# Two-layer graph attention kernel: row statistics moved between engines, and the bias row fed to the matmul as bf16 parts

## The chip, the cores and the metric

The kernel runs on one core of one Trainium2 chip. The metric is the device time of one execution in microseconds, the median of several runs. A core has five engines that work side by side, each through its own list of instructions in order: TensorE (PE in the profile, with its weight loads as PEld), VectorE (DVE), ScalarE (ACT), GpSimd (POOL) and SyncE (SP), which issues DMAs. Engines wait for one another through semaphores.

## The reference

`x` is 2048 x 256, `adj` is a 2048 x 2048 matrix of zeros and ones, sparse except for its first rows. Both layers have 8 heads of 32 columns.

```python
def _layernorm(x, axis=-1, eps=1e-05):
    m = jnp.mean(x, axis=axis, keepdims=True)
    v = jnp.var(x, axis=axis, keepdims=True)
    return (x - m) / jnp.sqrt(v + eps)
...
# layer 0
scores = jnp.einsum('hnd,hmd->hnm', q, k)
scores = jnp.where(adj > 0, scores, NEG_FILL)
attn = jax.nn.softmax(scores, axis=-1)
out = jnp.einsum('hnm,hmd->hnd', attn, vv)
...
# layer 1
h = (x @ W_w.T + W_b).reshape(Bn, H, D)
e = jax.nn.leaky_relu(s_src[:, None, :] + s_dst[None, :, :], negative_slope=0.2)
e = jnp.where(adj[:, :, None] == 0, jnp.float32(-1000000000.0), e)
attn = jax.nn.softmax(e, axis=1)
h_prime = jnp.einsum('ijh,jhd->ihd', attn, h).reshape(Bn, H * D)
return jax.nn.elu(h_prime)
...
x = _layernorm(x + _L0_gnn_ref(x, L0_gnn_x2, L0_gnn_v, adj), axis=-1)
x = _layernorm(x + _L1_gnn_ref(x, adj, L1_gnn_W_w, L1_gnn_W_b, L1_gnn_a), axis=-1)
```

What the change touches is the statistics of the two LayerNorms and the bias `W_b` in the projection `h`.

## The kernel before

The kernel never builds the dense attention. It turns `adj` into lists of edges, gathers for each edge the row of its neighbour, and adds the weighted rows up with matmuls against 0/1 selection matrices. The 2048 rows are 16 tiles of 128, taken in 7 groups; `k` from 0 to 15 is a tile's place in that order. A tile's edges are cut into chunks of 128 edges, 78 chunks in all. VectorE extracts the lists (`MAX8` on L1381, and the lines around it), GpSimd issues one indirect DMA per chunk (L965) into a ring of buffers of 24 slots in layer 0 and 44 in layer 1, VectorE scores and weighs the gathered rows (L1510, L1514, L1566), and TensorE sums them into a tile's rows (L1313). Layer 1 gathers from a table in memory that layer 0 writes. So its first gather waits for the last tile of layer 0 to be stored, while the lists are used again.

What a tile of layer 0 does when its sums are there (`tile_stages`, L314): VectorE divides by the softmax denominators (L1350, L1352), adds `x` (L1573), takes mean and variance with two statistics instructions (L1342, L1344) and adds eps to the variance (L1577). GpSimd raises that to the power -0.5 and forms the shift -mean * rstd (L983, L985). ScalarE writes the normed rows (L1134). TensorE turns them (L1319), ScalarE copies them out (L1141), and TensorE projects them: two instructions for the bias row times a row of ones (L1326), then four for the two halves of the weights (L1328); one source line of fp32 matmul shows as two instructions. ScalarE evacuates (L1148), SyncE stores to the table (L907), GpSimd adds to a column sum and splits the source scores in three bf16 parts (L1025 to L1039).

A tile of layer 1: divide, ELU on ScalarE (L1152, L1155), VectorE finishes the ELU (L1587), adds `x` (L1589) and takes the two statistics instructions; for every pair of tiles ScalarE makes a first guess of rstd (L1162, L1164), VectorE refines it in four small instructions (L1597 to L1603), ScalarE emits the two tiles (L1170).

The order of the work on each engine is fixed when the program is built. `all_stages` (L202) names some 1160 stages, each with an engine, a time in us, a rank and the stages it follows; `Order.flat` (L162) plays this list through once, always taking the startable stage of lowest rank, and every engine's program is written in the order that comes out. A changed time in a `put` can move any stage behind it, on all engines.

At the start SyncE loads the weights in 22 DMAs after the first four tiles of `adj` (L888 to L897), the bias row as one of them (L893); TensorE multiplies them (`sum_w`, L1229, L1231) when all have landed, and ScalarE copies the result (L1118, L1119), among it the last columns of `b_row`. The tile `e_w_sb` that held the weights is not used after that.

Of the kernel before, what the change touches and what calls it, by code (L numbers as in the profile page):

```python
# [14 lines left out]
P = 128  # L15
H = 8
# [185 lines left out]
def all_stages(plan):  # L202
# [111 lines left out]
    def tile_stages(layer, k, rank):  # L314
        end = last_sums(layer, k)
        if layer == 0:
            put("DVE", 2.1, rank - 0.2, ("norm", k), end, ("x", plan.group_of_k(k)), ("normed", k - 4) if k >= 4 else None)
            put("POOL", 1.1, rank - 0.3, ("shift", k), ("norm", k))
# [3 lines left out]
            put("PE", 2.0, rank - 0.2, ("project", k), ("copy_norm", k), ("evac", k - 1) if k else ("copy_mean", 0))  # L322
# [3 lines left out]
        else:  # L326
            put("DVE", 0.7, rank - 0.2, ("norm_a", k), end, ("emit", k - 4) if k >= 4 else ("normed", NK - 4 + k))
            put("ACT", 0.9, rank - 0.3, ("elu", k), ("norm_a", k), ("norm_b", k - 2) if k >= 2 else None)
            put("DVE", 1.6, rank - 0.2, ("norm_b", k), ("elu", k))
            if k % 2:  # L330
                put("ACT", 0.5, rank - 0.3, ("guess", k // 2), ("norm_b", k))
                put("DVE", 0.8, rank - 0.3, ("refine", k // 2), ("guess", k // 2))
# [347 lines left out]
def edge_pass(nc, x, adj, kv, w_nat, wT, w_b, a, out, table, needed, out_stored):  # L680
# [15 lines left out]
    with ExitStack() as ctx:  # L696
        def sb(name, shape, dt=F32):
            return ctx.enter_context(nc.sbuf_tensor(name, shape, dt))
# [24 lines left out]
        w_sb = sb("e_w_sb", [P, 2, C])  # L723
        w_ext = sb("e_w_ext", [P, 2, CX])
        b_row = sb("e_b_row", [1, CX])
# [69 lines left out]
        stats = sb("e_stats", [P, 6])  # L795
        mv = sb("e_mv", [P, 4, 2])
# [72 lines left out]
        def _(sp):  # L869
# [23 lines left out]
            sp.dma_start(b_row[:, 0:CV].rearrange("p (h e) -> p h e", e=D1)[:, :, 0:D], w_b.rearrange("(a h d) -> a h d", a=1, d=D)).then_inc(s("w_loaded"), 16)  # L893
# [22 lines left out]
        def _(pool):  # L916
# [35 lines left out]
            for stage in stages:  # L952
# [25 lines left out]
                elif stage[0] == "shift":  # L978
# [3 lines left out]
                    at_least(pool, "normed", k - 3)  # L982
                    own.did(nc.gpsimd.tensor_tensor(rstd[:, one], var_eps[:, one], minus_half[:], ALU.pow))  # L983
                    own.wait()
                    nc.gpsimd.tensor_scalar(shift[:, one], mv[:, k % 4, 0:1], rstd[:, one], -1.0, ALU.mult, ALU.mult).then_inc(s("shift_ready"), 1)  # L985
# [58 lines left out]
        def _(act):  # L1044
# [3 lines left out]
            for stage in stages:  # L1048
# [66 lines left out]
                elif stage[0] == "copy_w":  # L1115
# [3 lines left out]
                    nc.scalar.copy(b_row[:, CV:CX], pj[0:1, 4 * H:6 * H]).then_inc(s("w_ready"), 1)  # L1119
# [4 lines left out]
                elif stage[0] == "exp":  # L1124
# [5 lines left out]
                    nc.scalar.activation(weight_t[0:CH, :], shifted[0:CH, :], ACT.Exp, scale=SCALE if layer == 0 else 1.0).then_inc(s("exp_ready"), 1)  # L1130
                elif stage[0] == "normed":
# [25 lines left out]
                elif stage[0] == "guess":  # L1157
# [3 lines left out]
                    act.wait_ge(s("var_ready"), NT + 2 * j + 2)  # L1161
                    own.did(nc.scalar.activation(log_var[:, two], mv[:, two, 1], ACT.Ln, bias=eps[:]))  # L1162
# [11 lines left out]
        def _(pe):  # L1174
            for stage in stages:
# [48 lines left out]
                elif stage[0] == "sum_w":  # L1224
                    pe.wait_ge(s("const_ready"), N_CONST)
                    pe.wait_ge(s("w_loaded"), 16 * (6 + 2 * H))
# [3 lines left out]
                    for o in range(2):  # L1230
                        last = nc.tensor.matmul(pj[0:1, 4 * H:6 * H], b_col[:, o:o + 1], a_diag[:, o, :], start=(o == 0), stop=(o == 1))  # L1231
# [89 lines left out]
                elif stage[0] == "project":  # L1321
# [4 lines left out]
                    nc.tensor.matmul(pj[:, 0:CX], ones[0:1, :], b_row[:], start=True, stop=False)  # L1326
# [10 lines left out]
        def _(dve):  # L1337
# [3 lines left out]
            def moments(k):  # L1341
                st.did(v.bn_stats(stats[:], y[:, k % 4, :]))  # L1342
                st.wait()
                return v.bn_aggr(mv[:, k % 4, :], stats[:])  # L1344
# [10 lines left out]
            for stage in stages:  # L1355
# [212 lines left out]
                elif stage[0] == "norm":  # L1568
# [81 lines left out]
```

## Time and profile before

| | |
|---|---|
| median of 3 runs | 498.96 us (497.28 to 499.59) |
| the profiled execution's own time | 500.55 us |
| its span, first to last instruction | 498.9 us |
| granted TensorE clock, mean | 0.714 of full |
| PE busy | 277.4 us, 56% |
| DVE busy | 314.6 us, 63% |
| ACT busy | 157.2 us, 32% |
| POOL busy | 239.6 us, 48% |
| PEld busy | 193.7 us, 39% |

The share of busy time is a mean over stages that differ: list extraction and layer 0 share the first 300 us, and the gathers and sums of layer 1 fill the rest. A granted clock of 1.0 is 2.4 GHz and of 0.5 is 1.2 GHz; means between the two are mixtures. Idle time in a view names what ended it; "remote" is a release for which the profile has no instruction on this core.

### The profile page before, as it was taken

How to read it: one execution, taken by the hardware profiler on the slowest of the kernel's cores; microseconds unless marked ns; L12 is line 12 of the kernel's file. 1: busy time of each engine (PE TensorE's matmuls, PEld its weight loads, DVE VectorE, ACT ScalarE, POOL GpSimd, SP SyncE). 2: the span in 40 equal slices, each digit the busy share in tenths (PEclk: the TensorE clock that was granted, in tenths of full speed). 3: DMA queues.
4: the chain of work that ended last, by engine and by line, in shares of the span. 5: the costliest groups of instructions: out<-in, count | busy, mean ns of one | idle time of the engine just before them, and what ended most of it. 6: DMA issues, size and time to landing. Idle time of an engine off the chain costs nothing.

```text
span 498.9 us, 5673 instructions
## 1 busy us (share of the span) xinstructions
PE 277.4 (56%) x1506; PEld 193.7 (39%) x1506; DVE 314.6 (63%) x870; ACT 157.2 (32%) x352; POOL 239.6 (48%) x383
## 2 busy tenths in 40 slices
PE   0338676447755865886898875230004535595680
PEld 0226443335433543654556543120003423373450
DVE  3997988999978996996836620300014345677773
ACT  6433745325343334233221222000010022535322
POOL 7453746572478574478461335777742726000000
PEclk9859785969566995797755975575555957676796
DMA  8886567275277233154022002444431424101001
GB/s 308 266 266 233 213 206 262 57 284 169 97 198 228 109 88 107 43 135 125 1 68 84 12 24 67 112 112 112 112 78 28 113 60 109 45 1 43 21 1 47
DMA packets 24484, 57.94 MB, mean 116 GB/s; under 512 B 6560, under 2 KB 14880, under 8 KB 22400
## 3 DMA queue, kind: packets, MB, share of 16 engines
q0 software_dynamic: 10032, 31.77, 22.9%
q1 hardware_dynamic: 14416, 25.76, 14.9%
q8 instruction: 13, 0.21, 0.2%
q14 instruction: 23, 0.19, 0.1%
HBM read 53.19 MB, written 4.33 MB: 115 GB/s over the span
## 4 chain that ended last, share of the span: by engine, by line
PE 20%; another core or an unknown queue 16%; DVE 12%; issue 7%; POOL 3%; ACT 3%; DVEq 0%; ACTq 0%; POOLq 0%
PE e_po L1313 10%; PE e_pj L1328 2%; DVE e_weighted L1566 2%; PE e_pj L1326 1%; PE e_po L1297 1%; ACT e_sel_edges L1109 1%; DVE e_stats L1342 1%; PE e_pt L1222 1%; PE e_pq L1257 1%; POOL e_ring L965 1%; DVE e_y L1352 1%; DVE e_y L1589 1%; DVE e_y L1587 1%; POOL e_rstd L983 1%
## 5 line engine op out<-in xcount | busy, mean ns | idle before, releaser
L1313 PE MATMUL e_po<-e_weighted,e_sel_edges 128*128 128x264 f32 x312 | 100.9, 483 | 17.1 <-DVE e_weighted L1566 13.7
L965 POOL DMA_INDIRECT e_ring<-table,e_col_i x78 | 74.0, 948 | 45.2 <-DVE e_weighted L1566 22.3
L965 POOL DMA_INDIRECT e_ring<-in_kv,e_col_i x78 | 77.9, 998 | 34.6 <-issue 20.6
L1313 PEld LDWEIGHTS e_po<-e_weighted,e_sel_edges 128*128 128x128 f32 x312 | 73.2, 243 | 38.9 <-DVE e_weighted L1566 19.3
L1109 ACT COPY e_sel_edges<-e_pt 128x512 f32<-128x512 f32 (+3 forms) x45 | 23.6, 524 | 98.2 <-remote 53.3
L1222 PE MATMUL e_pt<-e_identb,e_sel_rows 128*128 128x128 bf16 x156 | 21.4, 273 | 44.9 <-ACT e_sel_edges L1109 31.1
L1566 DVE TENSOR_TENSOR e_weighted<-e_ring,e_pc 128x528 f32<-128x528 f32 (+1 forms) x55 | 35.6, 684 | 14.6 <-PE e_po L1313 9.5
L1257 PE MATMUL e_pq<-e_parts,e_sel_rows 128*128 128x256 bf16 x234 | 43.7, 351 | 1.0 <-DVE e_prod L1510 1.0
L1297 PE MATMUL e_po<-e_mean_row,e_diagonal 128*128 128x264 f32 x64 | 24.4, 474 | 35.3 <-issue 21.4
L1381 DVE MAX8 e_raw<-e_vals 128x8 bf16<-128x256 bf16 (+1 forms) x88 | 41.5, 513 | 1.0
L1222 PEld LDWEIGHTS e_pt<-e_identb,e_sel_rows 128*128 128x128 bf16 x156 | 14.1, 120 | 54.3 <-issue 52.5
L1053 ACT ACTIVATE e_vals<-e_adj 128x2048 bf16<-128x2048 int32 x16 | 30.6, 1911 | 14.5 <-DVE e_raw L1381 7.2
L1510 DVE TENSOR_TENSOR e_prod<-e_pq,e_ring 128x512 f32<-128x512 f32 (+1 forms) x40 | 25.6, 672 | 14.5 <-PE e_pq L1257 9.0
L1257 PEld LDWEIGHTS e_pq<-e_parts,e_sel_rows 128*128 128x128 bf16 x234 | 28.0, 124 | 10.2 <-DVE e_prod L1510 1.1
L1350 DVE RECIPROCAL e_rden<-e_po 128x8 f32<-128x8 f32 x32 | 6.5, 204 | 40.2 <-remote 32.6
L1297 PEld LDWEIGHTS e_po<-e_mean_row,e_diagonal 128*128 128x128 f32 x64 | 12.3, 222 | 39.6 <-issue 37.9
L1514 DVE TENSOR_REDUCE e_score<-e_prod 128x16 f32<-128x512 f32 (+1 forms) x40 | 24.9, 663 | 0.1
L1366 DVE TENSOR_TENSOR e_vals<-e_vals,e_code 128x2048 bf16<-128x2048 bf16 x16 | 19.5, 1219 | 8.1 <-ACT e_vals L1053 8.0
L983 POOL TENSOR_TENSOR e_rstd<-e_var_eps,e_minus_half 128x1 f32<-128x1 f32 x16 | 9.9, 618 | 30.4 <-DVE e_var_eps L1577 28.0
L1566 DVE TENSOR_TENSOR e_weighted<-e_ring,e_pl 128x528 f32<-128x528 f32 (+1 forms) x25 | 16.5, 688 | 9.6 <-PE e_po L1313 5.8
L1076 ACT ACTIVATE e_diagonal<-e_ident,e_filled 128x128 f32<-128x128 f32 x32 | 12.4, 395 | 19.2 <-issue 8.8
L1134 ACT ACTIVATE e_xres<-e_y,e_shift,e_rstd 128x256 f32<-128x256 f32 x16 | 9.6, 598 | 24.4 <-POOL e_shift L985 24.4
(184 smaller groups left out, 534.0 us busy)
## 6 DMA issues: line engine op xcount, KB each, us to landing
e_adj<-in_adj SPq DMA_DIRECT2D x16, 1024.0 KB
table<-e_hx SPq DMA_DIRECT2D x16, 136.0 KB
e_ring<-in_kv SPq DMA_DIRECT2D x1, 2112.0 KB, 13.1
out<-e_prod SPq DMA_DIRECT2D x16, 128.0 KB, 1.7
e_ring<-in_kv,e_col_i POOLq DMA_INDIRECT x78
e_ring<-table,e_col_i POOLq DMA_INDIRECT x78
e_xres<-in_x SPq DMA_DIRECT2D x2, 512.0 KB
e_xres<-in_x SPq DMA_DIRECT2D x3, 256.0 KB, 12.0
```

The costliest lines, as they stand in the source:

```text
L965: nc.gpsimd.indirect_dma_start(out=rings[layer][:, q % RING[layer], :], out_offset=None, in_=kv if layer == 0 else table, in_offset=bass.I ...
L1053: nc.scalar.activation(vals[:, k % 2, :], adj_tile[:, k % 2, :], ACT.Sign, accum_out=signs[:, k:k + 1]).then_inc(s("sgn_ready"), 1)
L1109: nc.scalar.copy(sel_edges[:, n % TURNED:n % TURNED + m, :].rearrange("p c r -> p (c r)"), pt[:, 0:m * P]).then_inc(s("turns_copied"), 1)
L1222: last = nc.tensor.matmul(pt[:, j * P:(j + 1) * P], sel(q + j), identb[:], start=True, stop=True)
L1257: last = nc.tensor.matmul(pq[b % 2][:, j * C:(j + 1) * C], sel(q0 + c0 + j), parts[:, g % 2, at, part, :], start=(part == 0), stop=(part = ...
L1297: nc.tensor.matmul(po[n % 2][:, 0:CV], diagonal[:, n % 2, :], mean_row[:], start=True, stop=False).then_inc(s("sums_begun"), 1)
L1313: nc.tensor.matmul(po[n % 2][:, 0:CV], sel_edges[:, (layer * plan.n_chunks + q) % TURNED, :], weighted[:, b % 3, j * CV:(j + 1) * CV], sta ...
L1366: st.did(v.tensor_tensor(tile_vals, tile_vals, code[:].bitcast(BF16), ALU.mult))
L1381: last = v.max(raw[:, i * TOP:(i + 1) * TOP], segs[:, i])
L1510: v.tensor_tensor(prod[:, i % 2, 0:m * C].rearrange("p (c k) -> p c k", c=m), pq[b % 2][:, 0:m * C].rearrange("p (c k) -> p c k", c=m), ri ...
L1514: ins = v.tensor_reduce(score[:, n % 2, c0:c0 + m, :].rearrange("p c h -> p (c h)"), by_head(prod[:, i % 2, 0:m * C]), AX_X, ALU.add)
L1566: v.tensor_tensor(weighted[:, b % 3, 0:m * CV].rearrange("p (c h d) -> p c h d", c=m, d=D1), rings[layer][:, at:at + m, lo:lo + CV].rearra ...
```

## The change

Layer norm. VectorE's add of `x` becomes a `scalar_tensor_tensor` that also gives the row sum (`accum_out`), and its two statistics instructions and the eps addition are gone. ScalarE gets a new stage per tile (`spread_of` in layer 0, `spread_of_b` in layer 1): it scales the sum to -mean, and squares `y - mean` with an accumulated row sum. The squared rows themselves go to a buffer that is free then. GpSimd's `shift` has one more small instruction in layer 0 (eps and the division by 256), before the power. `refine` on VectorE keeps four instructions.

Bias. The bias row is loaded on three partitions instead of one (three DMAs for one), `sum_w` makes its last columns on three partitions, and a new GpSimd stage `split_b` replaces the three copies by three bf16 parts whose sum is the fp32 row. The buffers for it lie in `e_w_sb`. In `project`, one bf16 matmul with a contraction over three partitions stands for the fp32 one with a contraction over one.

Planned times of the stages that changed are edited with it.

```diff
     def tile_stages(layer, k, rank):
         end = last_sums(layer, k)
         if layer == 0:
-            put("DVE", 2.1, rank - 0.2, ("norm", k), end, ("x", plan.group_of_k(k)), ("normed", k - 4) if k >= 4 else None)
-            put("POOL", 1.1, rank - 0.3, ("shift", k), ("norm", k))
+            put("DVE", 1.35, rank - 0.2, ("norm", k), end, ("x", plan.group_of_k(k)), ("normed", k - 4) if k >= 4 else None)
+            put("ACT", 1.0, rank - 0.3, ("spread_of", k), ("norm", k), ("project", k - 2) if k >= 2 else None)
+            put("POOL", 1.4, rank - 0.3, ("shift", k), ("spread_of", k))
...
-            put("PE", 2.0, rank - 0.2, ("project", k), ("copy_norm", k), ("evac", k - 1) if k else ("copy_mean", 0))
+            put("PE", 1.6, rank - 0.2, ("project", k), ("copy_norm", k), ("evac", k - 1) if k else ("copy_mean", 0))
...
-            put("DVE", 1.6, rank - 0.2, ("norm_b", k), ("elu", k))
+            put("DVE", 1.05, rank - 0.2, ("norm_b", k), ("elu", k))
+            put("ACT", 1.0, rank - 0.3, ("spread_of_b", k), ("norm_b", k))
             if k % 2:
-                put("ACT", 0.5, rank - 0.3, ("guess", k // 2), ("norm_b", k))
+                put("ACT", 0.5, rank - 0.3, ("guess", k // 2), ("spread_of_b", k))
...
     put("ACT", 0.7, 0.0, ("copy_w",), ("sum_w",))
+    put("POOL", 1.7, 0.0, ("split_b",), ("copy_w",))
...
-            sp.dma_start(b_row[:, 0:CV].rearrange("p (h e) -> p h e", e=D1)[:, :, 0:D], w_b.rearrange("(a h d) -> a h d", a=1, d=D)).then_inc(s("w_loaded"), 16)
+            for p in range(3):
+                sp.dma_start(b_row[p:p + 1, 0:CV].rearrange("p (h e) -> p h e", e=D1)[:, :, 0:D], w_b.rearrange("(a h d) -> a h d", a=1, d=D)).then_inc(s("w_loaded"), 16)
...
                     pool.wait_ge(s("var_ready"), k + 1)
                     at_least(pool, "normed", k - 3)
+                    own.did(nc.gpsimd.tensor_scalar(var_eps[:, one], squares[:, one], 1.0 / C, EPS, ALU.mult, ALU.add))
+                    own.wait()
                     own.did(nc.gpsimd.tensor_tensor(rstd[:, one], var_eps[:, one], minus_half[:], ALU.pow))
                     own.wait()
-                    nc.gpsimd.tensor_scalar(shift[:, one], mv[:, k % 4, 0:1], rstd[:, one], -1.0, ALU.mult, ALU.mult).then_inc(s("shift_ready"), 1)
+                    nc.gpsimd.tensor_tensor(shift[:, one], neg_mean[:, one], rstd[:, one], ALU.mult).then_inc(s("shift_ready"), 1)
+                elif stage[0] == "split_b":
+                    pool.wait_ge(s("w_ready"), 3)
+                    own.did(nc.gpsimd.tensor_scalar(less[:, 0:1], part_no[0:3, :], 0.5, -1.0, ALU.is_gt, ALU.mult))
+                    own.did(nc.gpsimd.tensor_scalar(less[:, 1:2], part_no[0:3, :], 1.5, -1.0, ALU.is_gt, ALU.mult))
+                    own.did(nc.gpsimd.memset(onesb, 1.0))
+                    for j in range(2):
+                        own.did(nc.gpsimd.tensor_copy(b_parts, b_row[:]))
+                        own.wait()
+                        own.did(nc.gpsimd.tensor_scalar(b_less, b_parts, less[:, j:j + 1], None, ALU.mult))
+                        own.wait()
+                        own.did(nc.gpsimd.tensor_tensor(b_row[:], b_row[:], b_less, ALU.add))
+                        own.wait()
+                    nc.gpsimd.tensor_copy(b_parts, b_row[:]).then_inc(s("bias_split"), 1)
...
+                elif stage[0] == "spread_of":
+                    k = stage[1]
+                    one = slice(k % 4, k % 4 + 1)
+                    act.wait_ge(s("z_ready"), k + 1)
+                    at_least(act, "h_summed", k - 1)
+                    if k == 1:
+                        act.wait_ge(s("rank_ready"), 1)
+                    own.did(nc.scalar.activation(neg_mean[:, one], total[:, one], ACT.Copy, scale=-1.0 / C))
+                    own.wait()
+                    nc.scalar.activation(xts[k % 2][:], y[:, k % 4, :], ACT.Square, bias=neg_mean[:, one], accum_out=squares[:, one]).then_inc(s("var_ready"), 1)
+                    act.wait_ge(s("var_ready"), k + 1)
+                elif stage[0] == "spread_of_b":
+                    k = stage[1]
+                    one = slice(k % 4, k % 4 + 1)
+                    act.wait_ge(s("z_ready"), NT + k + 1)
+                    own.did(nc.scalar.activation(neg_mean[:, one], total[:, one], ACT.Copy, scale=-1.0 / C))
+                    own.wait()
+                    nc.scalar.activation(elu[:, k % 2, :], y[:, k % 4, :], ACT.Square, bias=neg_mean[:, one], accum_out=squares[:, one]).then_inc(s("var_ready"), 1)
+                    act.wait_ge(s("var_ready"), NT + k + 1)
...
-                    nc.tensor.matmul(pj[:, 0:CX], ones[0:1, :], b_row[:], start=True, stop=False)
+                    if k == 0:
+                        pe.wait_ge(s("bias_split"), 1)
+                    nc.tensor.matmul(pj[:, 0:CX], onesb, b_parts, start=True, stop=False)
...
-            def moments(k):
-                st.did(v.bn_stats(stats[:], y[:, k % 4, :]))
-                st.wait()
-                return v.bn_aggr(mv[:, k % 4, :], stats[:])
+            def with_x(k):
+                return v.scalar_tensor_tensor(out=y[:, k % 4, :], in0=y[:, k % 4, :], scalar=1.0, in1=xres[:, k, :],
+                                              op0=ALU.mult, op1=ALU.add, accum_out=total[:, k % 4:k % 4 + 1])
...
-                    st.did(v.tensor_tensor(y[:, k % 4, :], y[:, k % 4, :], xres[:, k, :], ALU.add))
-                    st.wait()
-                    st.did(moments(k))
-                    st.wait()
-                    v.tensor_scalar(var_eps[:, k % 4:k % 4 + 1], mv[:, k % 4, 1:2], EPS, None, ALU.add).then_inc(s("var_ready"), 1)
+                    with_x(k).then_inc(s("z_ready"), 1)
...
-                    st.did(v.tensor_tensor(y[:, k % 4, :], y[:, k % 4, :], xres[:, k, :], ALU.add))
-                    st.wait()
-                    moments(k).then_inc(s("var_ready"), 1)
-                    dve.wait_ge(s("var_ready"), NT + k + 1)
+                    with_x(k).then_inc(s("z_ready"), 1)
```

## Rows read from the trace of the kernel before

**Rows 1.** The page's chain of work that ended last, shares by line

```profile
PE e_po L1313 10%; PE e_pj L1328 2%; DVE e_weighted L1566 2%; PE e_pj L1326 1%; PE e_po L1297 1%; ACT e_sel_edges L1109 1%; DVE e_stats L1342 1%; PE e_pt L1222 1%; PE e_pq L1257 1%; POOL e_ring L965 1%; DVE e_y L1352 1%; DVE e_y L1589 1%; DVE e_y L1587 1%; POOL e_rstd L983 1%
```

**Rows 2.** Stretches: length, busy us (instructions) by engine, then clock, DMA share, GB/s

```profile
50.00:200.00 150.00, 92.49 (x620) 63.87 (x617) 131.16 (x348) 66.14 (x139) 89.00 (x118) 0.75 0.52 168
...
250.00:275.00 25.00, 21.90 (x109) 14.44 (x109) 11.89 (x23) 5.15 (x12) 9.41 (x18) 0.50 0.27 76
275.00:304.00 29.00, 22.88 (x117) 14.66 (x117) 11.83 (x34) 8.55 (x21) 9.52 (x28) 0.79 0.06 20
304.00:422.00 118.00, 37.55 (x148) 27.09 (x146) 29.06 (x71) 12.16 (x31) 73.61 (x78) 0.60 0.36 93
422.00:499.00 77.00, 43.09 (x158) 30.54 (x158) 51.19 (x149) 28.85 (x74) 0.35 (x1) 0.72 0.09 28
```

**Rows 3.** Timeline (start us, length us), layer 1: a late release and POOL's two ring waits

```profile
351.47 0.21 DVE L1350 RECIPROCAL e_rden<-e_po 128x8 f32<-128x8 f32 x1 [26.15 <-remote]
...
382.28 0.94 POOL L965 DMA_INDIRECT e_ring<-table,e_col_i  x1 [13.22 <-DVE e_weighted L1566]
...
410.16 0.94 POOL L965 DMA_INDIRECT e_ring<-table,e_col_i  x1 [8.19 <-DVE e_weighted L1566]
```

**Rows 4.** Timeline of VectorE: the add of x, and what starts when its norm ends

```profile
214.19 0.43 DVE L1573 TENSOR_TENSOR e_y<-e_y,e_xres 128x256 f32<-128x256 f32 x1
...
215.41 0.21 DVE L1350 RECIPROCAL e_rden<-e_po 128x8 f32<-128x8 f32 x1
...
222.48 0.42 DVE L1573 TENSOR_TENSOR e_y<-e_y,e_xres 128x256 f32<-128x256 f32 x1
...
487.32 0.42 DVE L1589 TENSOR_TENSOR e_y<-e_y,e_xres 128x256 f32<-128x256 f32 x1
...
488.46 0.43 DVE L1587 SCALAR_TENSOR_TENSOR e_y<-e_prod,e_y 128x256 f32<-128x256 f32 x1
```

**Rows 5.** Groups of instructions: busy us, mean ns of one, idle before and releaser

```profile
L1491 DVE SCALAR_TENSOR_TENSOR e_hit<-e_slot_e,e_rel 128x256 f32<-128x256 f32 x16 | 8.3, 517 | 1.5 <-ACT e_slot_e L1098 0.4
L1491 DVE DVE_READ_ACCUMULATOR e_hit<-e_slot_e,e_rel 128x1 f32 x16 | 1.3, 81 | 0.0
L1059 ACT ACTIVATE e_half<-e_signs 128x2 f32<-128x2 f32 (+2 forms) x7 | 1.4, 197 | 0.1
L1152 ACT ACTIVATE e_left<-e_y 128x256 f32<-128x256 f32 x16 | 6.6, 413 | 27.9 <-DVE e_y L1352 27.9
L1053 ACT ACTIVATION_READ_ACCUMULATOR e_vals<-e_adj 128x1 f32 x16 | 3.0, 188 | 0.0
L985 POOL TENSOR_SCALAR e_shift<-e_mv,e_rstd 128x1 f32<-128x1 f32 x16 | 5.4, 339 | 1.6
L1029 POOL TENSOR_TENSOR e_h_sum<-e_h_sum,e_hx 128x264 f32<-128x264 f32 x15 | 11.6, 773 | 0.0
```

**Rows 6.** Timeline of TensorE around the projection of one tile, clock 0.5

```profile
245.94 1.49 PE L1257 MATMUL e_pq<-e_parts,e_sel_rows 128*128 128x256 bf16 x6
247.36 1.30 PE L1326 MATMUL e_pj<-e_b_row,e_ones 1*128 1x280 f32 x2
248.58 2.24 PE L1328 MATMUL e_pj<-e_w_ext,e_xt 128*128 128x280 f32 x4
```

**Rows 7.** Pieces of the chain that ended last: start us, us, what

```profile
231.72 1.27 PE e_pj L1326 x2
...
283.81 0.70 PE e_pj L1326 x2
```

**Rows 8.** Timeline of the start: weight loads and who waits for them

```profile
17.96 2.98 SPq L893 DMA_DIRECT2D e_b_row<-in_w_b  x1
...
28.09 0.42 SPq L897 DMA_DIRECT2D e_a_diag<-in_a  x1
...
32.47 1.86 PE L1229 MATMUL e_pj<-e_a_diag,e_w_sb 128*128 128x16 f32 x8 [8.47 <-DMA e_a_diag<-in_a]
...
40.67 1.63 POOL L1001 TENSOR_SCALAR e_flags<-e_rel 128x128 bf16<-128x128 f32 x1 [7.05 <-DVE e_rel_end L1468]
```

More of the change, by code:

```diff
@@ L723, in edge_pass @@
         w_sb = sb("e_w_sb", [P, 2, C])
+        w_flat = w_sb[0:3].rearrange("p k c -> p (k c)")
+        b_less = w_flat[:, 0:CX]
+        b_parts = w_flat[:, CX:CX + CX // 2].bitcast(BF16)
+        onesb = w_flat[:, CX + CX // 2:CX + CX // 2 + P // 2].bitcast(BF16)
+        less = w_flat[:, 2 * C - 2:2 * C]
         w_ext = sb("e_w_ext", [P, 2, CX])
-        b_row = sb("e_b_row", [1, CX])
+        b_row = sb("e_b_row", [3, CX])
         b_col = sb("e_b_col", [P, 2])
@@ L794, in edge_pass @@
         xts = [sb("e_xt", [P, C]), count0]
-        stats = sb("e_stats", [P, 6])
-        mv = sb("e_mv", [P, 4, 2])
+        norms = sb("e_norms", [P, 3, 4])
+        total, neg_mean, squares = norms[:, 0, :], norms[:, 1, :], norms[:, 2, :]
         var_eps = sb("e_var_eps", [P, 4])
@@ L1118, in _ @@
                         nc.scalar.copy(w_ext[:, k, CV:CX], pj[:, k * 2 * H:(k + 1) * 2 * H]).then_inc(s("w_ready"), 1)
-                    nc.scalar.copy(b_row[:, CV:CX], pj[0:1, 4 * H:6 * H]).then_inc(s("w_ready"), 1)
+                    nc.scalar.copy(b_row[:, CV:CX], pj[0:3, 4 * H:6 * H]).then_inc(s("w_ready"), 1)
                 elif stage[0] == "copy_mean":
@@ L1160, in _ @@
                     act.wait_ge(s("const_ready"), N_CONST)
-                    act.wait_ge(s("var_ready"), NT + 2 * j + 2)
-                    own.did(nc.scalar.activation(log_var[:, two], mv[:, two, 1], ACT.Ln, bias=eps[:]))
+                    own.did(nc.scalar.activation(log_var[:, two], squares[:, two], ACT.Ln, bias=eps[:], scale=1.0 / C))
                     own.wait()
@@ L1225, in _ @@
                     pe.wait_ge(s("const_ready"), N_CONST)
-                    pe.wait_ge(s("w_loaded"), 16 * (6 + 2 * H))
+                    pe.wait_ge(s("w_loaded"), 16 * (8 + 2 * H))
                     for k in range(2):
@@ L1230, in _ @@
                     for o in range(2):
-                        last = nc.tensor.matmul(pj[0:1, 4 * H:6 * H], b_col[:, o:o + 1], a_diag[:, o, :], start=(o == 0), stop=(o == 1))
+                        last = nc.tensor.matmul(pj[0:3, 4 * H:6 * H], b_col[:, o:o + 1].to_broadcast([P, 3]), a_diag[:, o, :], start=(o == 0), stop=(o == 1))
                     last.then_inc(s("w_summed"), 1)
@@ L1596, in _ @@
                     dve.wait_ge(s("guess_ready"), j + 1)
-                    st.did(v.scalar_tensor_tensor(out=guessed[:, two], in0=mv[:, two, 1], scalar=EPS, in1=guess[:, two], op0=ALU.add, op1=ALU.mult))
+                    st.did(v.scalar_tensor_tensor(out=guessed[:, two], in0=squares[:, two], scalar=C * EPS, in1=guess[:, two], op0=ALU.add, op1=ALU.mult))
                     st.wait()
-                    st.did(v.scalar_tensor_tensor(out=guessed[:, two], in0=guessed[:, two], scalar=-0.5, in1=guess[:, two], op0=ALU.mult, op1=ALU.mult))
+                    st.did(v.scalar_tensor_tensor(out=guessed[:, two], in0=guessed[:, two], scalar=-0.5 / C, in1=guess[:, two], op0=ALU.mult, op1=ALU.mult))
                     st.wait()
@@ L1602, in _ @@
                     st.wait()
-                    v.scalar_tensor_tensor(out=shift[:, two], in0=mv[:, two, 0], scalar=-1.0, in1=rstd[:, two], op0=ALU.mult, op1=ALU.mult).then_inc(s("refined"), 1)
+                    v.tensor_tensor(shift[:, two], neg_mean[:, two], rstd[:, two], ALU.mult).then_inc(s("refined"), 1)
                     dve.wait_ge(s("refined"), j + 1)
```

## The prediction, made blind

> **What bounds the kernel now.** I read the page first: VectorE is busiest, and no engine is near its span. The chain of waits shows no single owner either; its largest line is the layer's sums on TensorE, L1313, with 10%, and the lines of this change (L1326, L1342, L983) have about 1% each [rows 1]. So I went by stretches. From 50 to 200 us VectorE is busy 131.16 of 150 us (87%) with the edge lists: it paces. From 250 to 304 it is TensorE, 21.90 of 25 us and then 22.88 of 29; the granted clock is 0.50 in the first part (1.2 GHz) and 0.79 in the second. From 304 to 422 GpSimd issues the 78 gathers of layer 1, 73.61 of 118 us, and the rest of that stretch is waiting. The tail, 422 to 499, is a mixture led by VectorE, 51.19 of 77 us (66%), with TensorE at 43.09 [rows 2]. In the gather stretch GpSimd stands twice for a free ring slot, 13.22 and 8.19 us, because VectorE's weighing is late; ahead of that VectorE stood 26.15 us for a release that the profile names remote [rows 3]. I can't explain that wait from the records, and it makes this stretch the least certain one.
>
> The profiled execution took 500.55 us: a span of 498.9 and 1.65 around it. The median of the runs is 498.96, 1.59 less. I sum against 500.55 and take 1.6 off at the end.
>
> **VectorE's part of the norm.** Before, layer 0 goes from the add's start at 214.19 to the next tile's reciprocal at 215.41: 1.22 us for the add, two statistics instructions and eps. Layer 1 takes 487.32 to 488.46, 1.14 us [rows 4]. After, one instruction stands there. The nearest is L1491, the same form and one accumulated output, 128x256 fp32: 0.517 with a read of 0.081 beside it, which I take together as 0.50 to 0.60; I use 0.50 [rows 5]. That saves 0.72 us per tile of layer 0 and 0.64 per tile of layer 1. Ten of the sixteen adds of layer 0 start by 222.48 [rows 4], where VectorE paces: 10 x 0.72 = 7.2, of which I count 70%, since VectorE was idle for 13% and some of the gain lands in such gaps: -5.0. Bounds: 0 and -7.2. In the tail VectorE's steps of layer 1 are on the chain: L1342 has 1% of it, about 5 us, which is some ten tiles at about the 0.43 of the add over the same 128x256 [rows 1, 4]. Eight tiles x 0.64 = -5.1, bounds 0 and -10.2 (all sixteen).
>
> **ScalarE's new step.** It waits for the add, scales the sum (0.197 by L1059), squares 128x256 (0.413 by L1152) and reads the accumulator (0.188 by L1053): 0.80, and 0.95 with the gaps. GpSimd has one more 128x1 instruction per tile of layer 0, 0.339 by L985 [rows 5]. One norm's latency in layer 0 so changes by +0.20 +0.41 +0.19 +0.34 -0.72 = +0.42, with a hand-over 0.5. The last six tiles of layer 0 lie where TensorE paces and their projection must end before layer 1 may gather. I let three of them show it and three show VectorE's gain: +1.5 -2.2 = -0.7. In layer 1 the first guess of rstd, one per pair of tiles, now waits for ScalarE's own two steps in place of VectorE's: 0.80 + hand-over against 0.64. I take 0.45 each for the last four pairs: +1.8. And 32 steps of 0.95 us (30.4 us) go in front of what ScalarE does for others: copies of turned edges, exponentials, evacuations. ScalarE is busy 66 of 150, 5 of 25, 29 of 77 us [rows 2], 20 to 44%. So a step meets other work of ScalarE about a third of the time, and I let a third of what it meets be on the path, as no engine owns more than that of the chain: 30.4/9 = +3.4. Bounds: 0, and +30.4 if every one is exposed. What waits behind the new step on ScalarE, while it waits for VectorE's add, are the list copies for VectorE and the selection matrices for TensorE; behind the guess, the emits alone.
>
> **Bias.** Around one projection at clock 0.5, six bf16 matmuls of 256 columns take 1.49 us, 0.25 each, and the two fp32 halves of the bias start 1.22 before the next, 247.36 to 248.58 [rows 6]. One bf16 matmul of 280 columns costs about 0.27: -0.95 per tile at this clock. On the chain there are six pairs of L1326 behind 230 us, five of 1.1 to 1.3 and one of 0.70, the first and that one shown in [rows 7]; at the higher clock I take -0.49. Sum 5 x 0.95 + 0.49 = -5.2, bounds 0 and -10 (six of them in full and the four before at 0.7).
>
> **Start.** Two more b_row DMAs stand on SyncE's list before the a_diag ones. The b_row row has 2.98 us, the a_diag row 0.42; TensorE waits 8.47 for the last a_diag, until 32.47 [rows 8]. I count the issue, 2 x 0.46 = +0.9; bounds 0 and 2 x 2.98 = +6.0. split_b is nine GpSimd instructions on three partitions; by the 128x264 row, 0.77 for a full-width one [rows 5], at most 4.3 us (three copies and two adds of 280 columns at 0.77, 3.9, and the rest small). It lies in GpSimd's wait of 7.05 us before 40.67 [rows 8]; if that cover is gone, up to +4.
>
> **Sum.** +0.9 -5.0 -0.7 -5.2 -5.1 +1.8 +3.4 = -9.9. 500.55 - 9.9 = 490.65, and 1.6 less is 489.1 us.
>
> **Rivals.**
> A, the other side: ScalarE becomes the pacer of each tile. Its program is in fixed order, and a step waiting for the add holds all behind it. At 0.95 a step, 20 of 32 exposed give +19.0 in place of +3.4, so the sum is -13.3 +19.0 = +5.7: 506.25 own, 504.7. The point from which it decides is 14 exposed steps (14 x 0.95 = 13.3). For it: every layer-0 step sits between list copies. Against: at most 44% busy.
> B, VectorE's savings are hidden: the lists in fact wait for DMA or ScalarE. Then start +0.9, bias -5.2 and +3.4 stay: -0.9, 498.1. Against: 87% busy [rows 2].
> C, the clock. 275 to 304 ran at 0.79, the 25 us before at 0.50 [rows 2]. With less work TensorE could stay at 0.50 there: 22.88 busy x (0.79/0.50 - 1) = 13.3 more, 80% of it on the path: +10.6, so 499.7. The Trainium skill, "TensorE: Matmul & The Clock Gate", section "Part 1: The HAM clock gate (the "warmup" mystery)", says that TensorE's clock is held down by default and raised by activity, by which less bias work would be a loss and not a gain. By this rule the time is that of C. The trace does not bear it out plainly: the clock is 0.50 where TensorE is 88% busy, and 0.72 in the tail with 56% [rows 2].
> D, the remote release. The order changes, and the 26.15 us wait may fall elsewhere; half of GpSimd's 21.4 us of ring waits [rows 3] goes (-10.7, 478.4) or comes again (+10.7, 499.8).
> That the change does not do what it says is small: one instruction for four on VectorE is in the diff.
>
> **How the numbers follow.** Chances: forecast 0.48, A 0.17, B 0.14, C 0.07, D downwards 0.09, upwards 0.05. The likeliest's own range is 482 to 495 (the bounds of the list stage, tail and ScalarE terms taken by half). The range over all cases is 476 to 504: the lower end takes in D's gain, the upper nearly all of A. What a measurement can tell from no change is about 0.5%, 2.5 us: 496.5 to 501.5. Faster: the forecast's 0.48, D's 0.09 and 0.04 of B, 0.61. Same: 0.09 of B, 0.03 of C, 0.03 of D upwards, 0.03 of A, 0.18. Slower: the other 0.14 of A, 0.04 of C, 0.02 of D, 0.01 of B, 0.21.
>
> **What would show it.** VectorE's groups: L1342, L1344, L1577 gone, one accumulating group of 32 at about 0.5. VectorE busy down by some 20 us, ScalarE's up by 26. The first layer-1 gather, at 304 before, near 294. L1326 at one instruction a tile, near 0.27 at clock 0.50. GpSimd's wait before its 40.67 instruction shorter and not its start later. In the tail, idle time of ScalarE before the square, and the guess released by ScalarE. I am wrong if the gather starts no earlier than 301, if ScalarE's new group is the releaser of waits on TensorE or VectorE that sum to over 10 us, or if the clock in the TensorE stretch falls to 0.5 throughout.

## The result: 475.1 us where 489.1 was forecast

The changed kernel took 475.12 us, median of four runs (472.72 to 479.47), where the kernel before took 498.66; the ratio is 0.954, interval 0.9465 to 0.9614. The direction was right. The size was not: the forecast was a gain of 9.9 us and the gain was 23.5, and 475.1 lies just below the stated range of 476 to 504. Its profiled execution took 475.88 us, with a span of 472.7. Here and below, times are medians of all executions of a kernel, while a ratio is taken over the fast executions alone, so that a difference of medians and a ratio can stand up to some 2 us apart.

The page of the changed kernel, busy time by engine and the chain of waits by line:

```profile
PE 259.2 (55%) x1490; PEld 184.4 (39%) x1490; DVE 294.7 (62%) x822; ACT 180.9 (38%) x448; POOL 249.1 (53%) x409
...
PE e_po L1355 11%; POOL e_ring L974 4%; PE e_pj L1372 3%; DVE e_weighted L1609 3%; PE e_pq L1299 3%; DVE e_raw L1424 3%; PE e_pj L1281 2%; DMA e_adj<-in_adj 1%; DVE e_score L1557 1%; ACT e_sel_edges L1133 1%; SPq L900 1%; POOL e_h_sum L1053 1%; ACT e_vals L1077 1%; DVE e_prod L1553 1%
```

VectorE is busy 294.7 us, 19.9 less than before. ScalarE has 180.9, 23.7 more, and TensorE 259.2, 18.2 less. The page's list of the chain has no line of the statistics or the bias any more. The projection (L1372) is still in it.

Stretches of the changed kernel (length; busy us and instructions of PE, PEld, DVE, ACT, POOL; then clock, DMA share, GB/s):

```profile
50.00:200.00 150.00, 98.57 (x644) 69.44 (x643) 132.89 (x353) 72.83 (x163) 94.36 (x128) 0.74 0.53 171
...
250.00:275.00 25.00, 18.51 (x79) 12.95 (x78) 14.28 (x33) 7.33 (x22) 6.41 (x18) 0.80 0.15 43
```

The list stage is as dense on VectorE as it was (132.89 of 150 us, 89%), as a stage would be that VectorE paces and that is over sooner. The 25 us that ran at 0.50 before run at 0.80 [rows 2]; they hold other work now, since layer 0 ends 17 us earlier.

Timeline of the same kernel at the places of the steps: GpSimd's first gather of layer 1, the two ring waits and the last gather:

```profile
286.94 1.06 POOL L974 DMA_INDIRECT e_ring<-table,e_col_i  x1 [0.89 <-DMA table<-e_hx]
...
365.25 0.95 POOL L974 DMA_INDIRECT e_ring<-table,e_col_i  x1 [13.37 <-DVE e_weighted L1609]
...
392.07 0.95 POOL L974 DMA_INDIRECT e_ring<-table,e_col_i  x1 [6.91 <-DVE e_weighted L1609]
...
403.75 0.94 POOL L974 DMA_INDIRECT e_ring<-table,e_col_i  x1 [0.30 <-issue]
```

The same two ends of the gather stretch in the kernel before:

```profile
304.13 1.04 POOL L965 DMA_INDIRECT e_ring<-table,e_col_i  x1 [0.90 <-DMA table<-e_hx]
...
421.41 0.95 POOL L965 DMA_INDIRECT e_ring<-table,e_col_i  x1 [0.30 <-issue]
```

The end of that span was at 498.9. So layer 0 gave 17.2 us, the gather stretch 0.5 (117.3 against 116.8), and the tail, which is what lies behind the last gather, 8.5 (77.5 against 69.0). These are two single executions whose spans differ by 26.2; the medians differ by 23.5. Of the two ring waits of [rows 3] the first stands as it stood, and the second is 1.3 us shorter.

The instructions that the change put in, from the groups (busy us, mean ns of one) and the timeline of the changed kernel. L1172 is the square in layer 1; the one in layer 0, L1164, has the same mean of 508:

```profile
L1386 DVE SCALAR_TENSOR_TENSOR e_y<-e_y,e_xres 128x256 f32<-128x256 f32 x32 | 14.1, 441 | 1.1
L1172 ACT ACTIVATE e_prod<-e_y,e_norms 128x256 f32<-128x256 f32 x16 | 8.1, 508 | 0.5
L1370 PE MATMUL e_pj<-e_w_sb 3*128 3x280 bf16 x16 | 5.5, 343 | 3.1 <-issue 2.9 <-ACT e_hx L1191 0.2
```

```profile
35.77 0.25 POOL L999 TENSOR_SCALAR e_w_sb<-e_part_no 3x1 f32<-3x1 f32 x1 [2.20 <-ACT e_b_row L1143]
...
41.15 1.37 POOL L1009 CAST e_w_sb<-e_b_row 3x280 bf16<-3x280 f32 x1
42.62 0.66 POOL L1025 TENSOR_SCALAR e_flags<-e_rel 128x128 bf16<-128x128 f32 x1
```

The add with its sum is 0.44 and 0.08 for the read, close to the 0.50 taken. ScalarE's square is 0.51, not 0.41. GpSimd's split of the bias row runs from 35.77 to 42.52, 6.75 us, not at most 4.3, and GpSimd's work behind it starts at 42.62 instead of 40.67 [rows 8].

### The profile page after: what moved, and what is told of

Its sections match the earlier page's. It is cut to its first block, busy times and chain, and to the rows that moved or that the text cites. A ratio compares the mean times of both kernels' runs of the same rounds, so it can differ in the third digit from the quotient of the medians.

```text
span 472.7 us, 5744 instructions
## 1 busy us (share of the span) xinstructions
PE 259.2 (55%) x1490; PEld 184.4 (39%) x1490; DVE 294.7 (62%) x822; ACT 180.9 (38%) x448; POOL 249.1 (53%) x409
## 3 DMA queue, kind: packets, MB, share of 16 engines
q1 hardware_dynamic: 14448, 25.77, 15.5%
## 4 chain that ended last, share of the span: by engine, by line
PE 25%; issue 19%; DVE 18%; POOL 11%; another core or an unknown queue 10%; ACT 8%; SPq 4%; DMA 2%; DVEq 1%; ACTq 0%; POOLq 0%
PE e_po L1355 11%; POOL e_ring L974 4%; PE e_pj L1372 3%; DVE e_weighted L1609 3%; PE e_pq L1299 3%; DVE e_raw L1424 3%; PE e_pj L1281 2%; DMA e_adj<-in_adj 1%; DVE e_score L1557 1%; ACT e_sel_edges L1133 1%; SPq L900 1%; POOL e_h_sum L1053 1%; ACT e_vals L1077 1%; DVE e_prod L1553 1%
## 5 line engine op out<-in xcount | busy, mean ns | idle before, releaser
L1355 PE MATMUL e_po<-e_weighted,e_sel_edges 128*128 128x264 f32 x312 | 98.7, 475 | 8.0 <-DVE e_weighted L1609 5.0
L974 POOL DMA_INDIRECT e_ring<-in_kv,e_col_i x78 | 79.2, 1016 | 34.1 <-issue 20.8
L1339 PE MATMUL e_po<-e_mean_row,e_diagonal 128*128 128x264 f32 x64 | 23.1, 450 | 41.0 <-issue 23.2
L1299 PE MATMUL e_pq<-e_parts,e_sel_rows 128*128 128x256 bf16 x234 | 42.7, 347 | 1.2 <-DVE e_prod L1553 0.9
L1264 PE MATMUL e_pt<-e_identb,e_sel_rows 128*128 128x128 bf16 x156 | 18.8, 246 | 34.3 <-ACT e_sel_edges L1133 17.0
L1299 PEld LDWEIGHTS e_pq<-e_parts,e_sel_rows 128*128 128x128 bf16 x234 | 28.4, 124 | 11.5 <-DVE e_prod L1553 1.9
L1339 PEld LDWEIGHTS e_po<-e_mean_row,e_diagonal 128*128 128x128 f32 x64 | 10.9, 205 | 46.2 <-issue 45.1
L1264 PEld LDWEIGHTS e_pt<-e_identb,e_sel_rows 128*128 128x128 bf16 x156 | 12.9, 111 | 40.5 <-issue 38.2
L1609 DVE TENSOR_TENSOR e_weighted<-e_ring,e_pl 128x528 f32<-128x528 f32 (+1 forms) x25 | 16.5, 689 | 8.6 <-PE e_po L1355 5.5
L1154 ACT ACTIVATE e_weight_t<-e_shifted 128x128 f32<-128x128 f32 (+5 forms) x14 | 4.3, 305 | 38.0 <-issue 30.8
L1195 ACT ACTIVATE e_left<-e_y 128x256 f32<-128x256 f32 x16 | 6.6, 415 | 29.8 <-DVE e_y L1395 28.3
```

Of the source, the lines that this page charges most:

```text
L974: nc.gpsimd.indirect_dma_start(out=rings[layer][:, q % RING[layer], :], out_offset=None, in_=kv if layer == 0 else table, in_offset=bass.I ...
L1264: last = nc.tensor.matmul(pt[:, j * P:(j + 1) * P], sel(q + j), identb[:], start=True, stop=True)
L1299: last = nc.tensor.matmul(pq[b % 2][:, j * C:(j + 1) * C], sel(q0 + c0 + j), parts[:, g % 2, at, part, :], start=(part == 0), stop=(part = ...
L1339: nc.tensor.matmul(po[n % 2][:, 0:CV], diagonal[:, n % 2, :], mean_row[:], start=True, stop=False).then_inc(s("sums_begun"), 1)
L1355: nc.tensor.matmul(po[n % 2][:, 0:CV], sel_edges[:, (layer * plan.n_chunks + q) % TURNED, :], weighted[:, b % 3, j * CV:(j + 1) * CV], sta ...
L1609: v.tensor_tensor(weighted[:, b % 3, 0:m * CV].rearrange("p (c h d) -> p c h d", c=m, d=D1), rings[layer][:, at:at + m, lo:lo + CV].rearra ...
```

## The experiments

Eighteen kernels ran in five groups (e1 to e4, e5 to e8, e9 to e12, e13 to e16, e17 and e18), each on a chip of its own together with the kernel before, and there were two levels of time. On three chips the kernel before took 493 to 497 us, on two others 436, with the same instructions; what differs is told in the last section. So each kernel is compared with the kernel before of its own group. The intervals of the ratios reach 0.3 to 0.7% to either side, 1.5 to 3 us.

**Order and instructions apart.** e1 is the kernel before with the changed kernel's list of stages. The new stages issue nothing:

```
-put("DVE", 2.1, ..., ("norm", k), ...)        # and the other planned times as changed
+put("DVE", 1.35, ..., ("norm", k), ...)
+put("ACT", 1.0, ..., ("spread_of", k), ("norm", k), ...)   # the stage issues nothing
```

> The order of the stages and the planned times of the changed kernel, every instruction as before (the new stages issue nothing). Before is 498.7, the changed kernel 475.1. Theory S (the shorter instructions are the gain, and were counted too small: the tail and TensorE's part show all of them): the order alone brings 0 to -3 us, 496 to 499. Theory O (the planner's new order brings what the forecast missed): -8 to -14 us, 485 to 491.

Measured 498.1 against 496.9, ratio 1.0001 (0.9958 to 1.0043): this order is worth nothing that can be seen to the old instructions. e2 has all changed instructions and the old planned times, with the new stages planned at zero:

```
-put("DVE", 1.35, ..., ("norm", k), ...)       # project 1.6 -> 2.0, norm_b 1.05 -> 1.6, shift 1.4 -> 1.1
+put("DVE", 2.1, ..., ("norm", k), ...)
-put("ACT", 1.0, ..., ("spread_of", k), ...)   # spread_of_b and split_b too
+put("ACT", 0.0, ..., ("spread_of", k), ...)
```

> All instructions of the changed kernel, in the order of the kernel before (planned times as before, the new stages planned at zero). Theory S: most of the gain is here, -20 to -24 us, 475 to 479. Theory O: -10 to -14 us, 485 to 489. If ScalarE's steps, now placed without the planner's knowledge, stand in others' way, it is above 489.

Measured 491.5, ratio 0.988 (0.9828 to 0.994). Neither theory holds; it is the third case of the expectation, above 489.

But e2 is not what its expectation calls it. A stage planned at zero still holds back what follows it, by the plan's 0.15 us from engine to engine and, in layer 0, by `project` of the tile two places before. When the lists of stages of the two kernels are played through as `Order.flat` does, 35 of ScalarE's 272 old stages stand elsewhere in e2 than before, 29 of VectorE's 295, 43 of TensorE's 322 and 15 of GpSimd's 217. Against the changed kernel it is 74, 55, 71 and 15. So e2 runs in a third order, and no run has the changed instructions in the order of the kernel before. What it shows is that the instructions lose most of their gain in this third order. e14 repeated it beside the changed kernel:

> The changed kernel, as reference for the next three on one chip. Where before is near 436 (no late releases): 0.961, 419 to 422. Where before is near 497: 0.954, 474 to 476.

> All changed instructions in the order of the kernel before. If the missing place for ScalarE's steps costs the 5 us that planning them at zero cost (425.5 against 420.9), and VectorE's and TensorE's shorter planned times nothing: about 5 us above the changed kernel, ratio 0.972. If the old planned times of VectorE and TensorE cost as well: 8 to 17 us above it, ratio 0.98 to 0.99.

The changed kernel took 476.0 against 496.8, ratio 0.959 (0.9532 to 0.9657), and e14 488.9, 0.987. The order that comes from the old planned times costs 12.9 us against the changed kernel's. Part of it is already there at ScalarE's cast of the fifteenth tile of `adj`, which feeds VectorE's lists; first e14, then e13:

```profile
184.85 1.91 ACT L1077 ACTIVATE e_vals<-e_adj 128x2048 bf16<-128x2048 int32 x1
```

```profile
175.75 1.91 ACT L1077 ACTIVATE e_vals<-e_adj 128x2048 bf16<-128x2048 int32 x1
```

The cast is 9.1 us later. The first gather of layer 1 is 6.8 us later (295.98 in e14 and 289.22 in e13), the gather stretch is 1.7 longer and the tail 3.8. e8 and e18 change only the planned time of ScalarE's two new steps in the changed kernel (56 of ScalarE's old stages move by it, and 54 of TensorE's):

```
-put("ACT", 1.0, rank - 0.3, ("spread_of", k), ...)      # and spread_of_b
+put("ACT", 0.0, rank - 0.3, ("spread_of", k), ...)
```

> The changed kernel with one planned time altered: ScalarE's new steps are planned at 0 instead of 1.0 us in both layers; every instruction and every other planned time as changed. If the lack of a place for ScalarE's steps is what made the changed instructions in the old order lose most of their gain (491.5 in place of 475): 483 to 492, and the last casts of adj on ScalarE 5 to 9 us later than in the changed kernel. If it was VectorE's and TensorE's old planned times: 475 to 478.

> The changed kernel with ScalarE's new steps planned at 0. Where before takes 436: 0.977 again. Where before takes 497: 0.968 to 0.972 (481 to 483) if the cost is 5 to 7 us there too, and 0.985 (488) if it is all that the old order costs.

e8 took 425.5 at the 436 level, ratio 0.977 (0.9714 to 0.9832); the changed kernel took 420.9 there (e9 below, another group), 4.6 less. e18 took 482.5 against 493.3 of the kernel before, ratio 0.979 (0.9749 to 0.982); beside it the changed kernel with one planned time altered (e17 below) took 476.8, 5.7 less. By the ratios both differences are about 7 us. So the order that comes of steps without a planned time costs some 5 to 7 of the 13 us. The rest goes with the other old planned times, which no run separated. The casts of `adj` were not late in e8, against what was expected (the fifteenth starts at 174.43, and at 173.87 in e9), nor in e18 (175.88, and 175.75 in e13), so the late cast of e14 does not come from this one planned time.

**The parts apart.** Bias alone and norm alone, each with its planned times (the other part's hunks of the diff undone):

> The bias part alone, its planned times with it; the norm as before. Theory S: TensorE's stretch gives back 0.95 us for each of six to eight tiles, less 1 us at the start: -5 to -8 us, 491 to 494. Theory O: between 0 and -3, the rest comes only with the norm. If the bias were free on TensorE: +1, 500.

> The norm part alone, its planned times with it; the bias as before. Theory S: -8 in the tail (13 tiles behind the last gather x 0.64) and -8 to -10 in layer 0: -16 to -19 us, 480 to 483. The forecast's own terms for this part (-5.0 -0.7 -5.1 +1.8 +3.4) would be -5.6, 493.

Bias alone 488.7, ratio 0.983 (0.9773 to 0.9894), -8.2 us. Norm alone 482.0, ratio 0.967 (0.961 to 0.9723), -14.9 us. The same two at the other level, with the changed kernel beside them:

> The changed kernel itself once more, beside the next three on one chip. In the last call the kernel before took 435.9 us and not 497 to 499: in those traces the long remote releases and GpSimd's two ring waits of layer 1 are absent. The parts measured there were -7.5 (norm in layer 0) and -3.3 (norm in layer 1). If the gain does not depend on the late releases: ratio 0.948 (-23 us). If part of it came from the way the late releases stack up: norm -10.8 and bias -8 add to -19, ratio 0.957.

> The norm part alone once more (482.0 against 496.9 before: -15). If the layers add up: -7.5 -3.3 = -10.8. If both together let the planner do more: -15 again.

> The bias part alone once more (488.7 against 496.9: -8.2), to stand beside the kernel with the bf16 bias in the last six tiles only (-5.1 in the last call) and in none (next). Expected -7 to -9.

The changed kernel took 420.9 against 436.0, ratio 0.961 (0.9541 to 0.968), -15.1 us. Norm alone took 425.1 (-10.9) and bias alone 429.1 (-6.9). At both levels the parts together come to 2 or 3 us more than the whole (-23.1 against -20.8, -17.8 against -15.1), which is no more than the intervals allow by chance. Each of these kernels also has an order of its own; for the bias the next runs show that it is worth nothing, for the norm no run tells its order from its instructions. Then the norm by layers:

> The norm part in layer 0 alone, planned times with it; layer 1 and the bias as before. The norm part in both layers took 15 us off (482.0 against 496.9), and its trace has the first gather of layer 1 9.5 us earlier and the stretch behind the last gather 6.8 us shorter. If the layers add up: -8 to -10 us, 487 to 489. If the layer-0 gain needs nothing but TensorE's stretch (the forecast's -5.7 less ScalarE's cost): -2 to -4, 493 to 495.

> The norm part in layer 1 alone, planned times with it. If VectorE paces the whole tail (13 or 14 norms behind the last gather x 0.64 us saved, ScalarE's steps hidden): -6 to -9 us, 488 to 491, first gather of layer 1 unmoved. If the forecast's sizes hold (-5.1 +1.8 and half of ScalarE's 3.4): -1.6, 495.

Layer 0 alone 428.4 against 435.9, ratio 0.983 (0.9776 to 0.9879), -7.5 us. Layer 1 alone 432.6, ratio 0.991 (0.9875 to 0.9937), -3.3 us. The sum, -10.8, agrees with the norm part's -10.9. And the bias by tiles, with the order fixed (`k >= 10` in e7, never in e12):

```
-nc.tensor.matmul(pj[:, 0:CX], onesb, b_parts, start=True, stop=False)
+if k >= 10:
+    nc.tensor.matmul(pj[:, 0:CX], onesb, b_parts, start=True, stop=False)
+else:
+    nc.tensor.matmul(pj[:, 0:CX], ones[0:1, :], b_row[0:1, :], start=True, stop=False)
```

> The bias-alone kernel (488.7 against 496.9 for before) in which the first ten tiles keep the fp32 bias matmul; order, DMAs and the three parts unchanged. If only the six late projections, where TensorE paces, gave the gain: as bias alone, 488 to 490. If the early ten gave their half too (10 x 0.35 to 0.9 us of TensorE): 492 to 494. If the gain is from the order that the shorter planned time brings: 488 to 489 too, and the next run (no tile changed) tells that from the first case.

> Order, planned times, three DMAs and GpSimd's split of the bias-alone kernel, but every tile keeps the fp32 bias matmul. If the order that the shorter planned time brings is a gain of its own: -3 us or more. If the gain is the matmul time: +0 to +3 us (the start costs 0.9 or more, the order nothing), and the three runs step down -5 from none to the last six and -3 from there to all sixteen.

None 436.1 against 436.0 (ratio 1.0019, 0.9978 to 1.006); the last six 430.8 against 435.9, -5.1 us; all sixteen -6.9. So the gain of the bias part is the matmul and not its order, which e12 shares. The six late tiles give most of it; what the ten early ones add, 1.8 us between two groups, is not clear of the intervals. The start with the split costs nothing that can be seen, which by e12's interval means less than 2.6 us.

**What ScalarE's time costs.** e15 takes each squared sum twice:

```
+own.did(nc.scalar.activation(xts[k % 2][:], y[:, k % 4, :], ACT.Square, ..., accum_out=squares[:, one]))
+own.wait()
 nc.scalar.activation(xts[k % 2][:], y[:, k % 4, :], ACT.Square, ..., accum_out=squares[:, one]).then_inc(...)
```

> The changed kernel in which ScalarE takes each squared sum twice (some 0.75 us more per tile, 24 us more in all; order and planned times unchanged). The forecast let a ninth of ScalarE's time be on the path: +2.7 us for this. If ScalarE's steps are hidden in full: 0 to +1. If they pace (the forecast's rival of the other sign): +10 to +24.

Measured 484.9 where the changed kernel took 476.0: +8.9 us. The page's busy line, e15 and then e13:

```profile
PE 264.8 (55%) x1490; PEld 187.6 (39%) x1490; DVE 295.9 (61%) x822; ACT 199.7 (41%) x512; POOL 250.7 (52%) x409
```

```profile
PE 260.5 (55%) x1490; PEld 185.8 (39%) x1490; DVE 296.6 (63%) x822; ACT 181.0 (38%) x448; POOL 249.9 (53%) x409
```

ScalarE is busy 18.7 us more, and nearly half of that shows (8.9 of 18.7), on an engine that is busy for 41% of the span. A ninth was forecast. The first gather is 3.4 us later than in e13 (292.60 against 289.22), and the tail 4.6 longer. In the tail two of VectorE's waits for ScalarE grew (in sum, times, longest), those for the guess of rstd and for the ELU, e15 (408 to 483 us) and then e13 (404 to 475):

```profile
DVE e_guessed L1637 <- ACT e_guess L1210: 5.9, 5, 2.2
DVE e_y L1630 <- ACT e_prod L1202: 3.8, 4, 1.9
```

```profile
DVE e_guessed L1633 <- ACT e_guess L1206: 2.0, 2, 1.5
DVE e_y L1626 <- ACT e_prod L1198: 1.8, 3, 1.3
```

Together they are 5.9 us more, so waits of this kind are enough to explain the longer tail.

**Other planned times.** e16 sets three planned times of the changed kernel nearer to its trace; e17 only the first of them:

```
-put("POOL", 1.7, 0.0, ("split_b",), ("copy_w",))        +put("POOL", 6.8, ...)     # e16 and e17
-put("DVE", 1.35, rank - 0.2, ("norm", k), ...)          +put("DVE", 1.2, ...)      # e16
-put("POOL", 1.4, rank - 0.3, ("shift", k), ...)         +put("POOL", 1.7, ...)     # e16
```

> The changed kernel with three planned times set to what its trace shows (split_b 6.8 us for 1.7, norm on VectorE 1.2 for 1.35, shift on GpSimd 1.7 for 1.4). If the order's sensitivity is general: 3 us or more either way. If only steps without any place matter: within 2 us of the changed kernel.

> The changed kernel with one planned time changed: split_b on GpSimd 6.8 us, as measured, in place of 1.7. If that one (GpSimd's block at 36 to 42 us, which the plan took for a quarter of it) made the 6 us: 469 to 471 where the changed kernel takes 476 (ratio 0.950), or 0.951 where before takes 436. If it was norm and shift: 0.958 to 0.961.

e16 took 469.8 us where the changed kernel took 476.0, ratio to before 0.950 (0.943 to 0.9564). It is the fastest version at this level, 27.0 us under before and 6.2 under the changed kernel. e17 took 476.8 against 493.3, ratio 0.963 (0.9587 to 0.9683). The split's planned time alone does not bring it; it is norm's or shift's, or a pair of changes together. Which of these is open. It is open too whether the gain comes from times nearer to the trace or from a lucky order: e16 moves 36 of ScalarE's and 51 of TensorE's old stages against the changed kernel, and the plan's own end is the same 423.1 us for the changed kernel, e16 and e17.

## Why the forecast was too small

The signs of the steps were right, and the sizes were too small. The step that failed is the sizing of the savings. At the level where the forecast was made, the norm part has the terms -5.0 -0.7 -5.1 +1.8 +3.4 = -5.6 and measured -14.9 (e4); start and bias have +0.9 -5.2 = -4.3 and measured -8.2 (e3). That is 9.3 and 3.9 of the 13.6 us by which the forecast fell short. Taken one by one:

*Norm in layer 0.* The terms are -5.0 and -0.7, with half of ScalarE's +3.4 against them: -4.0. Measured -7.5 at the 436 level (e5; its interval is 5.3 to 9.8). Here two things made the term small: the discount "of which I count 70%" on the ten early tiles, and the late six, of which only three were to show a gain and three a loss. Sixteen tiles at 0.72 are 11.5 us. Which of the two was wrong was not separated.

*Norm in layer 1.* The terms are -5.1 and +1.8 and the other half of ScalarE's cost, -1.6. Measured -3.3 at the 436 level (e6). At the level of the forecast the tail alone fell by 8.5 us in the profiled executions, and by 6.8 with the norm part alone (411.12 to 481.8 in e4). There twelve adds of `x` start behind the last gather; the first is

```profile
426.49 0.42 DVE L1589 TENSOR_TENSOR e_y<-e_y,e_xres 128x256 f32<-128x256 f32 x1
```

and the last at 488.92. Twelve savings of 0.64 are 7.7; eight were counted. The eight came from the chain's 1% for L1342, read as ten tiles of the tail. The chain has that line fifteen times, five of them in layer 0 and nine behind the last gather; three of the twelve tiles there are not on it at all. The full number does not close the gap: with twelve tiles the term would be -4.2 where the tail of e4 gave 6.8. The rest may be in the prices of ScalarE's steps or in the scatter of single executions. At the 436 level only six adds stand behind the last gather; in e12, the gather and the first of them:

```profile
391.39 0.95 POOL L972 DMA_INDIRECT e_ring<-table,e_col_i  x1 [0.30 <-issue]
...
400.76 0.43 DVE L1618 TENSOR_TENSOR e_y<-e_y,e_xres 128x256 f32<-128x256 f32 x1
```

Six savings of 0.64 are 3.8, near the 3.3 measured.

*Bias, -5.2 for six tiles.* Six tiles gave 5.1 in e7. That match is partly luck: it is from the 436 level, and at the level of the forecast the whole part gave 8.2. The ten earlier tiles, put at nothing, gave at most a few us; no run has them at that level.

*Start, +0.9.* Right in its trace: `sum_w` starts at 33.29 instead of 32.47. In the time it cannot be seen (e12, ratio 1.002), and +0.9 lies within that interval. The split overran its estimate because instructions were miscounted. It has ten, not nine, and seven of them run over 280 columns, not five: the two multiplications were left out, which took 1.01 and 0.99 us, and the last cast took 1.37.

*ScalarE, +3.4.* A ninth of its added time was to show. Of the further 18.7 us in e15 nearly half did. At that rate its 23.7 us more would cost 11 us; that the first 23.7 cost as much was not measured. If they did, the gross saving was about 32 us (20.8 + 11), and that is more than the 29.9 by which VectorE (19.9) and the bias matmul (15.5 before, 5.5 after) were relieved. So the rate is likely lower for the first part, or a wait went as well. The true price is open.

*The level.* At 436 the gain is 15.1 us, at the level where the forecast was made 20.8 (e13) and 23.5. The ratios, 0.961 and 0.959, are the same within their intervals, so it is not shown that the level added to the gain in its own right. Rival D put its change into GpSimd's ring waits, and those hardly moved: 13.22 and 8.19 before, 13.37 and 6.91 after.

The other rivals. A, ScalarE as the pacer: added time on ScalarE does cost (e15), and its price did not exceed the savings. B, savings hidden: excluded by e4 and e5. C, the clock: the changed kernel's 275 to 304 ran at 0.74, but the gathers begin at 287; the 12 us up to there ran at 0.86 and the 25 before at 0.80. The 54 us ahead of the first gather ran at 0.66 before and at 0.81 after. So less work did not bring the lower level. By the rule that the prediction cites from the Trainium skill, "TensorE: Matmul & The Clock Gate", section "Part 1: The HAM clock gate (the "warmup" mystery)", it would have been a loss; no run here shows one. What nobody forecast is the opposite, that a higher clock in this stretch is part of the gain. That is not excluded: the same 54 us ran at 0.72 in e1, at 0.78 in e13, at 0.71 in e4 and at 0.85 in e3. At the 436 level it was 0.82 in e12, which takes the time of the kernel before, and 0.78 in e9, so there the gain came without it. Single executions of the kernel before at mean clocks of 0.713, 0.721 and 0.724 had spans of 495.2, 498.8 and 492.2, so the mean over the span does not order the times.

Of the signs named beforehand: VectorE down by 20 and ScalarE up by 26 were right (19.9, 23.7); the gather was expected near 294 and came at 286.94; one bias instruction of 0.27 at the low clock was 0.34 in the mean over all; GpSimd's start behind the split was later, against the forecast. None of the three signs of being wrong came: the gather started before 301, no wait of TensorE or VectorE is put down to ScalarE's new squares (GpSimd's are, four of 15.5 us in sum), and the clock did not fall to 0.5. They guarded against a loss, and no sign was named for a gain far larger than forecast.

## What to carry to other kernels

Where one engine leads a stretch, work out what is taken off it in full as well, for every tile that the stretch holds, and count the tiles from the timeline and not from their share of the chain. Here the full sum for the norm was 21.8 us (16 x 0.72 and 16 x 0.64), the discounted one with ScalarE's costs 5.6, and the measured gain 14.9. Work moved to an engine that is 40% busy is not free: in e15 each added microsecond on ScalarE cost about half a microsecond. And where the order is laid out from planned times, a changed planned time is a changed order on every engine. At the slower level the same instructions gained 5 to 8 us with the old planned times, 11 with ScalarE's new steps planned at nothing, 16.5 in e17, 21 to 23.5 with the plan of the change and 27 in e16. A run meant to hold the order fixed has to be compared stage by stage with the order that it is to keep.

## What was not expected of the hardware

The same program took 493 to 497 us on three chips and 436 on two (the first measurement, 498.7, belongs to the slower level). In the traces of the slower level several waits end long after the instruction that they wait for by the records; at the other level these are gone, and GpSimd's 78 gathers of layer 1 run without a pause. VectorE's first division of layer 1, whose eight chunks of sums have ended by 311 us in both, in the changed kernel at the slower level and at the faster one (e9):

```profile
333.73 0.21 DVE L1393 RECIPROCAL e_rden<-e_po 128x8 f32<-128x8 f32 x1 [25.89 <-remote]
```

```profile
309.54 0.21 DVE L1393 RECIPROCAL e_rden<-e_po 128x8 f32<-128x8 f32 x1 [3.17 <-PE e_po L1355]
```

The wait is nearly the same in every kernel of that level where the profile shows it: 26.15 in before [rows 3], 26.13 in e1, 25.59 in e4, 24.04 in e15, 23.73 in e13. The stage from the first to the last gather takes 115 to 118 us in the kernels of the slower level and 96.6 to 97.3 in those of the other. The tail is longer with it: 77.5 us before and 41.8 in e12, because six more tiles are left for it. The last gather and the end with them lie at 403.75 and 472.7 in the changed kernel; without, in e9, the last gather is here, and the end at 418.1:

```profile
381.71 0.95 POOL L974 DMA_INDIRECT e_ring<-table,e_col_i  x1 [0.30 <-issue]
```

What makes the releases late on some chips was not found, and no run tried it by itself. A forecast in us from a profile that contains such waits holds for that level alone; as a ratio (0.959 and 0.961) the gain of this change was the same at both within the intervals.
